# Decoder on one Trainium2 core: row sends spaced out, routing of the last two batches in a stage of its own, x transposed in place, one of five block copies on VectorE

## The chip, the cores and the metric

The kernel runs on one core of one Trainium2 chip. The metric is the device time of one execution, in microseconds (us). The engines are TensorE (PE for matmuls, PEld for weight loads), VectorE (DVE), ScalarE (ACT), GpSimd (POOL) and SyncE (SP, which here only issues DMAs).

## The reference

Two decoder layers with post-layernorm on x of 8 x 512 x 256, float32. The last attention and the mixture of experts, around which the change turns, are:

```python
# layer 0: x = LN(x + attn(x)); x = LN(x + cross(x, ctx)); x = LN(x + butterfly_ffn(x))
# layer 1: x = LN(x + causal_rope_attn(x)); x = LN(x + xattn(x, ctx)); x = LN(x + moe(x))
# xattn: 8 heads of 64; keys and values of x (512) and of ctx (64) joined: 576 keys
sim = jnp.einsum('bihd,bjhd->bhij', q1, k) * scale
attn = jax.nn.softmax(sim, axis=-1)
out = jnp.einsum('bhij,bjhd->bihd', attn, v)
return out.reshape(B, N1, h * d) @ Wo + bo
# moe: 8 experts, the best 2 of each row
xn = (x - mu) * jax.lax.rsqrt(var + EPS) * gamma + beta
logits = jnp.einsum('btd,ed->bte', xn, router_w)
probs = jax.nn.softmax(logits / TEMP, axis=-1)
w, idx = jax.lax.top_k(probs, K)
h = jax.nn.silu(jnp.einsum('btd,edf->betf', xn, W1))
y = jnp.einsum('betf,efd->betd', h, W2)
out = jnp.einsum('bte,betd->btd', wdense, y)      # wdense: softmax weight of the chosen two, else 0
return out + res
```

## The kernel before

x of all eight batches stays in SBUF for the whole kernel (`sh.x_all`, 32 tiles of 128 rows x 256). The stages run one after the other, each a block whose engines all meet at its end: a0 (self attention with decay), x0 (`cross_attention_heads`), f0 (`butterfly_ffn`), a1 (causal attention with rotation), x1 (the last attention), `route`, `experts`, `combine`. a0, a1 and x1 are three kinds of one function, `attention`.

**Steps of x1.** A batch has U = 8 steps: two groups of four heads (G = 2) times four tiles of 128 query rows. Each step handles one tile of one group. TensorE computes its scores (line 878, keys of x, and line 888, keys of ctx); VectorE takes the maximum and moves them to SBUF (lines 1270 and 1279); ScalarE takes the exp, a step later (L1074); TensorE transposes the exps block by block (L901, and L904 for the ctx keys), three steps later (LAG_T); they are copied from PSUM to SBUF, and TensorE multiplies them with the values four steps later (L922, L925) into x_O. In x1 a head has five blocks of transposes per step (T_UNIT = 5: four of 128 keys and one of 64), and ScalarE copies all five (L1065). In a0 and a1 there are four blocks, and VectorE copies one of them (L1254).

**The end of a group.** The reciprocals of the sums are transposed by TensorE (L938), copied to rows by VectorE (L1201), written to DRAM and read back, spread over the partitions, by SP (L697, `x_invrep`). At the group's last step VectorE multiplies x_O with x_invrep (L1261, once per group; the one of group 1 of batch b - 1 falls into batch b's early steps, that of group 0 at step 7). Values of the next group are computed at the same place (L814, L823), copied by ScalarE (L1044). The output product is L837, the layernorm L151. Because of the lags, batch b's last products come in batch b + 1's early steps; after the last batch there is a tail of six steps with nothing of its own.

**x in.** TensorE transposes x (L749 in attention) out of a buffer `xin`, into which SP copies the next batch from `x_all` (512 KB) at step 0 (L703); x0 does the same.

**Routing in x1.** Class `Routing`. Batch b - 2 is routed during batch b (b >= 2): `choose` normalises its rows on VectorE (L298), GpSimd scales them by gamma and beta in place (L372, L375), VectorE takes 32 dot products of a row tile with an expert's router row (L306, four tiles x eight experts), the best two (L314 onwards); `tally` counts them on TensorE; `locate` turns counts into slots (L343 to L356) and releases `placed` (L355). Then `send` issues eight indirect DMAs (L382), each writing 128 rows of `xn` to the slots of `moe_sent`. There is one buffer `xn`, so the next batch's normalising waits until the eight sends have arrived. GpSimd's queue is this loop and nothing else: scale b, send b, scale b + 1, ... for b = 0 to 6. The order on VectorE is that of a generator: `advance(routed[1])` runs one piece of the routing at set places of the steps.

**Tail and route.** Batch 6 is chosen in x1's tail, and located behind it (`advance(ro.locate(...))` at the end of attention). `route` does batch 7: choose (L2029 is its first instruction), tally, locate, send; then it computes each expert's tiles and the slots to gather from, while SP loads the experts' weights (16 transfers of 1 MB, L2007 and L2008). `experts` fetches its first rows at L2136 and multiplies from L2166 on.

## Time and profile before

| | us |
|---|---|
| runs | 4067.27, 4079.03, 4083.48 |
| median | 4079.03 |
| profiled execution | 4074.16, its span 4072.4 |

| stage | from | to | us |
|---|---|---|---|
| a0 | 0 | 835 | 835 |
| x0 | 835 | 1090 | 255 |
| f0 | 1090 | 1336 | 246 |
| a1 | 1336 | 2409 | 1073 |
| x1 | 2409 | 3300 | 891 |
| route | 3300 | 3370 | 70 |
| experts | 3370 | 3953 | 583 |
| combine | 3953 | 4072 | 119 |

Over the span TensorE is busy 3337.6 us (82%), its weight loads 2459.7 (60%), VectorE 2328.9 (57%), ScalarE 1891.7 (46%) and GpSimd 953.4 (23%); the mean granted clock of TensorE is 0.919. The loads of `xin` are 16 transfers of 512 KB in a0 and a1 (4.4 us from issue to landing), and 16 in x0 and x1 (4.2 us).

How to read the views: a row of the timeline has the start (us), the duration (us), engine and line, the operation, output<-inputs, their shapes, the number of instructions in the row, and in brackets the idle time of the engine ahead of it with what ended it: "<-remote" names no instruction, "<-issue" means that the profile shows nothing that was waited for, "<-PEq" TensorE's sequencer. SPq and POOLq are DMA issues. A row of busy time by window has the window, its length, then PE, PEld, DVE, ACT and POOL busy time, each with its count of instructions, the granted TensorE clock (PEclk, as a share of full speed), the mean busy share of the DMA engines, and GB/s. Names begin with the stage (x_ is x0's or x1's, a_ is a0's or a1's, moe_ is the routing's).

### The profile page before, as it was taken

To read this page: it belongs to the slowest core of one execution; us is meant where nothing else is said; L and a number is where in the kernel's file an instruction comes from. 1 tells how busy PE (TensorE), PEld (TensorE's weight loads), DVE (VectorE), ACT (ScalarE), POOL (GpSimd) and SP (SyncE) were. 2 spreads that over 40 slices of the span, in tenths; PEclk is the share of its full clock that TensorE was granted. 3 is DMA by queue.
4 is the path that set the end of the run, shared out by engine and by line. 5 is a ranking of instruction groups with operands and counts; after the bars stand their busy time and mean duration, and the time that the engine had idled before them with its cause. 6 is when DMAs were issued, how large, how long until landed. Compare 5 with 4: busy or idle time off the path is not lost. (4 is left out here: it accounts for less than half of the span.)

```text
span 4072.4 us, 74256 instructions
## 1 busy us (share of the span) xinstructions
PE 3337.6 (82%) x25588; PEld 2459.7 (60%) x25588; DVE 2328.9 (57%) x7554; ACT 1891.7 (46%) x4610; POOL 953.4 (23%) x758
## 2 busy tenths in 40 slices
PE   5888888857699588889889869998888818999970
PEld 3656565647678366666566646776666616776750
DVE  4777777769777356565666634566666652222226
ACT  4777878723332255555555526554555501112110
POOL 0000000034100576676666700011011120000014
PEclk9999999978799799999999979999999969999995
DMA  3111111010200222122221220000000041111113
GB/s 117 53 68 67 67 54 65 7 48 21 97 1 1 82 64 56 48 58 57 58 56 49 55 68 12 18 27 28 28 28 23 22 174 47 33 33 34 34 41 109
DMA packets 115308, 204.35 MB, mean 50 GB/s; under 512 B 23744, under 2 KB 66176, under 8 KB 110080
## 3 DMA queue, kind: packets, MB, share of 16 engines
q1 hardware_dynamic: 104048, 148.21, 12.5%
q0 software_dynamic: 10896, 51.39, 3.4%
q8 instruction: 216, 3.54, 0.4%
q14 instruction: 148, 1.21, 0.1%
HBM read 91.92 MB, written 57.28 MB: 37 GB/s over the span
## 5 line engine op out<-in xcount | busy, mean ns | idle before, releaser
L1074 ACT ACTIVATE a_t<-a_t,a_neg 128x512 f32<-128x512 f32 (+3 forms) x1024 | 642.7, 633 | 9.4 <-DVE a_neg L1284 8.4
L901 PE MATMUL a_T<-ident,a_t 128*128 128x128 f32 x3328 | 512.0, 288 | 126.8 <-ACT a_pT L1065 57.1
L901 PEld LDWEIGHTS a_T<-ident,a_t 128*128 128x128 f32 x3328 | 384.1, 146 | 324.1 <-issue 291.4
L1065 ACT ACTIVATE a_pT<-a_T 128x512 f32<-128x512 f32 (+3 forms) x768 | 370.6, 512 | 273.0 <-PE a_T L901 272.9
L1279 DVE CUSTOM_DVE_ANT_0 a_t<-a_A,a_decay 128x512 f32<-128x512 f32 x512 | 323.0, 687 | 100.6 <-PE a_A L866 100.5
L1279 DVE CUSTOM_DVE_ANT_0 a_t<-a_A,a_table 128x384 f32<-128x384 f32 (+3 forms) x512 | 220.9, 486 | 165.6 <-PE a_A L878 164.3
L1115 POOL TENSOR_TENSOR a_rsin<-a_rawswapped,a_sin 128x512 f32<-128x512 f32 x128 | 168.9, 1319 | 561.0 <-DMA a_rawswapped<-a_raw 547.6
L2236 DVE COPY experts_y<-experts_Y 128x256 f32<-128x256 f32 x72 | 30.5, 424 | 438.2 <-PE experts_Y L2174 438.2
L2186 PE MATMUL experts_H<-ex_w,experts_xgT 128*128 x576 | 261.8, 597 | 0.8 <-ACT experts_xgT L2213 0.6
L2174 PE MATMUL experts_Y<-ex_w,experts_hT 128*128 x1152 | 260.5, 379 | 1.0 <-DVE experts_hT L2245 1.0
L1065 ACT ACTIVATE x_pT<-x_T 128x512 f32<-128x512 f32 (+1 forms) x320 | 178.5, 593 | 169.1 <-PE x_T L901 149.7
L2174 PEld LDWEIGHTS experts_Y<-ex_w,experts_hT 128*128 128x128 f32 x1152 | 218.8, 190 | 61.3 <-issue 35.2
L1279 DVE CUSTOM_DVE_ANT_0 x_t<-x_A,x_table,x_mx 128x512 f32<-128x512 f32 x256 | 177.6, 747 | 133.4 <-PE x_A L878 132.7
L2277 POOL DMA_INDIRECT combine_got<-moe_results,moe_fetch x64 | 62.2, 972 | 628.8 <-PEq L2255 593.0
L1254 DVE COPY a_pT<-a_T 128x512 f32<-128x512 f32 (+3 forms) x256 | 148.2, 579 | 94.3 <-PE a_T L901 92.9
L2219 ACT ACTIVATE experts_h<-experts_H 128x512 f32<-128x512 f32 x144 | 86.0, 597 | 241.1 <-PE experts_H L2186 241.1
L1074 ACT ACTIVATION_READ_ACCUMULATOR a_t<-a_t,a_neg 128x1 f32 x1024 | 196.6, 192 | 0.0
L1074 ACT ACTIVATE x_t<-x_t,x_neg 128x576 f32<-128x576 f32 x256 | 194.7, 765 | 0.0
L837 PE MATMUL a_A<-a_wo,a_oT 128*128 128x256 f32 x640 | 166.4, 413 | 31.7 <-DVE a_mx L1279 22.9
L382 POOL DMA_INDIRECT moe_sent<-moe_xn,moe_place x64 | 62.9, 983 | 495.0 <-issue 424.3
L922 PEld LDWEIGHTS a_O<-a_pT,a_v 128*64 128x64 f32 x2560 | 138.2, 137 | 66.5 <-ACT a_pT L1065 41.3
L878 PE MATMUL a_A<-a_khl,a_qhl 64*128 64x128 f32 (+3 forms) x1536 | 157.3, 336 | 22.2 <-POOL a_khl L1125 19.1
(297 smaller groups left out, 6853.3 us busy)
## 6 DMA issues: line engine op xcount, KB each, us to landing
moe_sent<-a_zeros POOLq DMA_DIRECT2D x33, 1024.0 KB, 8.4
a_rawswapped<-a_raw SPq DMA_DIRECT2D x512, 64.0 KB, 2.0
a_invrep<-a_inv_dram SPq DMA_DIRECT2D x64, 256.0 KB, 4.0
ex_w<-in_f_w_dram SPq DMA_DIRECT2D x16, 1024.0 KB
experts_xg<-moe_sent SPq DMA_DIRECT2D x72, 128.0 KB, 2.0
moe_results<-experts_y SPq DMA_DIRECT2D x72, 128.0 KB, 1.7
a_xin<-x_all SPq DMA_DIRECT2D x16, 512.0 KB, 4.4
x_xin<-x_all SPq DMA_DIRECT2D x16, 512.0 KB, 4.2
```

The lines of the kernel that those rows point to most:

```text
L837: mm = pe.matmul(bank[:, 0:D], oT[:, t, qt * P:(qt + 1) * P], wo[:, t, :], start=(t == 0), stop=(t == n_o - 1))
L878: mm = pe.matmul(A[seg.bank(at)][:, 0:keys(u)], q_hl[r, gp, ql, j // 2, q], k_hl[r, gp, kl_, j // 2, 0:keys(u)], start=(n == 0), stop=(n = ...
L901: mm = pe.transpose(bank[:, kt, :], t_of(u, j, kt * P, (kt + 1) * P), sh.ident[:])
L922: mm = pe.matmul(O[pr][64 * half:64 * half + 64, q], v_sb[:, kt, col], p_tile(u, j, kt), start=(kt == 0), stop=last, skip_group_check=True)
L1065: nc.scalar.activation(to, of, ACT.Copy).then_inc(t_empty, 1)
L1074: nc.scalar.activation(t_of(u_e % U, j, 0, n), t_of(u_e % U, j, 0, n), ACT.Exp, bias=neg[:, slot, j:j + 1], scale=SCALE, accum_out=total[: ...
L1115: nc.gpsimd.tensor_tensor(rsin[:], raw_swapped[:, n % 2, :], sin[:], ALU.mult).then_inc(sin_done, 1)
L1254: nc.vector.tensor_copy(p_tile(u, 3, 0, kts), bank[:, 0:kts, :] if kts > 1 else bank[:, 0, :])\
L1279: nc.vector.tensor_tensor_reduce(t_of(s, j, 0, n), A[seg.bank(name)][:, 0:n], table[:, at:at + n], 1.0, mx1[:, slot, j:j + 1] if x1 else L ...
L2174: mm = pe.matmul(Y[parity][:], hT[:, f, :], w2[:, bass.ds(e, 1), f, :].rearrange("p a d -> p (a d)"), start=(f == 0), stop=(f == FT - 1))
L2186: mm = pe.matmul(H[half][:], xgT[:, dt, :], w1[:, bass.ds(e, 1), dt, half * 512:(half + 1) * 512] .rearrange("p a f -> p (a f)"), start=(d ...
L2219: nc.scalar.activation(h[:, half * 512:(half + 1) * 512], H[half][:], ACT.Silu).then_inc(h_act, 1)
```

## The change

**Sends.** `send` is split into `scale` and a `send` of one group of 128 rows. `xn` has two buffers. GpSimd's loop in x1 is now: scale b, then the eight sends of b - 1, one by one, send g only when the exps have come to a set count (`exped >= ((b + 2) * U + 2) * 4 + 3 * g`, so three heads' exps further for each). Batches 0 to 4 are sent in x1.

**Last two batches.** Batch 6 is no longer routed in x1 (`route = x1 and own and b >= 2`, and no `locate` behind the tail). `route` first sends batch 5's rows, then handles 6 and 7 together: it normalises eight tiles into a buffer `xhat`, GpSimd scales them into `rows` (the memory of the router rows), TensorE transposes `xhat` (32 blocks), ScalarE applies gamma and beta while copying (4 instructions of 512 columns), 16 matmuls with eight columns of output give the logits; the slots come from prefix sums in log rounds; sixteen sends follow. Three small loads (gamma, beta, the transposed router) go ahead of the weight loads.

**x in place.** The buffers `xin`, their loads and the waits for them go in a0, a1, x1 and x0; TensorE transposes straight from `x_all`.

**Copies.** In x1 VectorE copies block 3 of five (512 columns, L1254); ScalarE copies the other four. The condition for a bank to be free counts ScalarE's and VectorE's copies apart.

```diff
-        if b:
-            wait_apart(dve, met, (self.arrived, 16 * self.G * b))
+        xn = self.xn[:, b % 2]
+        if b > 1:
+            wait_apart(dve, met, (self.arrived, 16 * self.G * (b - 1)))
...
-    def send(self, pool, met, b):
-
-        nc, G = self.nc, self.G
-        wide = [P, QT, D]
+    def scale(self, pool, met, b, to, xn):
+
+        nc, wide = self.nc, [P, QT, D]
         wait_apart(pool, met, (self.normal, b + 1))
-        nc.gpsimd.tensor_tensor(self.xn[:], self.xn[:], self.gamma[:].unsqueeze(1).to_broadcast(wide),
-                                ALU.mult).then_inc(self.scaled, 1)
+        nc.gpsimd.tensor_tensor(to, xn, self.gamma[:].unsqueeze(1).to_broadcast(wide), ALU.mult).then_inc(self.scaled, 1)
         wait_apart(pool, met, (self.scaled, b + 1))
-        nc.gpsimd.tensor_tensor(self.xn[:], self.xn[:], self.beta[:].unsqueeze(1).to_broadcast(wide),
-                                ALU.add).then_inc(self.rows, 1)
-        wait_apart(pool, met, (self.placed, b + 1))
-        if b:
-            pool.wait_ge(self.arrived, 16 * G * b)
-        for g in range(G):
-            at = b * G + g
-            pool.indirect_dma_start(self.sent, bass.IndirectOffsetOnAxis(ap=self.place[:, at:at + 1], axis=0),
-                                    self.xn[:, g // TOP, :], None).then_inc(self.arrived, 16)
+        nc.gpsimd.tensor_tensor(to, to, self.beta[:].unsqueeze(1).to_broadcast(wide), ALU.add).then_inc(self.rows, 1)
+
+    def send(self, pool, b, g, row):
+
+        at = b * self.G + g
+        pool.indirect_dma_start(self.sent, bass.IndirectOffsetOnAxis(ap=self.place[:, at:at + 1], axis=0),
+                                row, None).then_inc(self.arrived, 16)
...
-                if s == 0 and nxt:
-                    sp.wait_ge(xt_done, b * DT + DT)
-                    sp.dma_start(xin[:], sh.x_all[:, bass.ds(b * QT + QT, QT), :]).then_inc(xin_in, 16)
...
-                            mm = pe.transpose(bank[:, qt * P:(qt + 1) * P], xin[:, qt, dt * P:(dt + 1) * P],
+                            mm = pe.transpose(bank[:, qt * P:(qt + 1) * P], sh.x_all[:, b * QT + qt, dt * P:(dt + 1) * P],
...
-                if x1 and qt == QT - 1 and b >= 2:
+                if x1 and qt == QT - 1 and 2 <= b < B:
...
-                free = [(t_empty, job + 1)] if x1 else \
-                    [(t_copied, ug + 1)] if j == 1 else [(t_empty, ug * 3 + (2, 0, 3, 4)[j])]
+                if x1:
+                    free = [(t_copied, ug + 1)] if j == 0 else [(t_empty, ug * 4 + (0, 2, 3, 4, 5)[j])]
+                else:
+                    free = [(t_copied, ug + 1)] if j == 1 else [(t_empty, ug * 3 + (2, 0, 3, 4)[j])]
...
-                    if do_t and j < (T_UNIT if x1 else 3):
+                    if do_t and j < T_UNIT and j != 3:
...
-                for b in range(B - 1):
-                    ro.send(pool, (ready, N_READY), b)
+                for b in range(B - 2):
+                    ro.scale(pool, (ready, N_READY), b, ro.xn[:, b % 2], ro.xn[:, b % 2])
+                    for g in range(Routing.G if b else 0):
+
+                        if g == 0:
+                            wait_apart(pool, (ready, N_READY), (ro.placed, b))
+                            if b > 1:
+                                pool.wait_ge(ro.arrived, 16 * Routing.G * (b - 1))
+                        pool.wait_ge(exped, ((b + 2) * U + 2) * 4 + 3 * g)
+                        ro.send(pool, b - 1, g, ro.xn[:, (b - 1) % 2, g // TOP, :])
...
-                route = x1 and b >= 2
+                route = x1 and own and b >= 2
...
-                if not x1 and s < U and (own if u_t >= 0 else prev):
+                if s < U and (own if u_t >= 0 else prev):
                     u = u_t % U
                     wait_apart(dve, (ready, N_READY), (pv, b * U + (u_t + 1)),
                                (t_full, (b * U + u_t) * T_UNIT + (4 + T_CREDIT)))
-                    kts, bank = keys(u) // P, T[(u * T_UNIT + 3) % 2]
+                    kts, bank = S // P if x1 else keys(u) // P, T[(u * T_UNIT + 3) % 2]
...
-                advance(ro.locate(nc.vector, routed[0], B - 2))
...
+        xhat = sb("xhat", [P, LQ, D])
+        rows = ro.router
...
+            pe.wait_ge(loaded, 16 * LOADS)
+            for b in range(LAST):
+                pe.wait_ge(ro.normal, FIRST + b + 1)
+                for dt in range(DT):
+                    for qt in range(QT):
+                        mm = pe.transpose(X[b * DT + dt][:, qt, :], xhat[:, b * QT + qt, dt * P:(dt + 1) * P], sh.ident[:])
+                    mm.then_inc(xt_full, 1)
+            for b in range(LAST):
+                pe.wait_ge(xt_done, (b + 1) * DT)
+                for qt in range(QT):
+                    for dt in range(DT):
+                        mm = pe.matmul(R[:, b * QT + qt, :], xn_T[:, b, dt, qt * P:(qt + 1) * P], router[:, dt, :],
+                                       start=(dt == 0), stop=(dt == DT - 1))
+            mm.then_inc(logits, 1)
+            pe.wait_ge(ro.chose, FIRST + 1)
+            of = chosen[:].rearrange("p g e -> p (g e)")
+            pe.matmul(BEFORE[:].rearrange("p g e -> p (g e)"), ro.tri[:], of, start=True, stop=True)
+            pe.matmul(TOTAL[:].rearrange("p g e -> p (g e)"), ro.ones[:], of, start=True, stop=True).then_inc(counted, 1)
 
         @block.scalar
         def _(act):
+            act.wait_ge(loaded, 16 * LOADS)
+            for b in range(LAST):
+                for dt in range(DT):
+                    act.wait_ge(xt_full, b * DT + dt + 1)
+                    nc.scalar.activation(xn_T[:, b, dt, :], X[b * DT + dt][:].rearrange("p a b -> p (a b)"), ACT.Identity,
+                                         bias=beta[:, dt:dt + 1], scale=gamma[:, dt:dt + 1]).then_inc(xt_done, 1)
             act.wait_ge(shifted, 1)
             nc.scalar.activation(ro.packed[:], ro.packed[:], ACT.Exp).then_inc(exped, 1)
 
         @block.gpsimd
         def _(pool):
             pool.wait_ge(ready, 1)
-            ro.send(pool, (ready, 1), B - 1)
+            wait_apart(pool, (ready, 1), (ro.placed, FIRST))
+            pool.wait_ge(ro.arrived, 16 * G * (FIRST - 1))
+            for g in range(G):
+                ro.send(pool, FIRST - 1, g, ro.xn[:, (FIRST - 1) % 2, g // TOP, :])
+            for b in range(LAST):
+                r = slice(b * QT, (b + 1) * QT)
+                ro.scale(pool, (ready, 1), FIRST + b, rows[:, r, :], xhat[:, r, :])
+            wait_apart(pool, (ready, 1), (ro.rows, B), (ro.placed, FIRST + 1))
+            for b in range(LAST):
+                for g in range(G):
+                    ro.send(pool, FIRST + b, g, rows[:, b * QT + g // TOP, :])
             pool.wait_ge(ro.arrived, 16 * GROUPS)
 
         @block.vector
         def _(dve):
             nv = nc.vector
-            nv.memset(ro.scratch[:], 0.0).then_inc(ready, 1)
+            nv.memset(scratch[:], 0.0).then_inc(ready, 1)
             dve.wait_ge(ready, 1)
             steps = ro.steps(dve, (ready, 1))
-            advance(ro.choose(dve, nv, sh.x_all, steps, (ready, 1), B - 1))
+            for t in range(LQ):
+                ins = nv.bn_stats(stats[:, t, :], sh.x_all[:, FIRST * QT + t, :])
+            steps.link(ins)
+            for t in range(LQ):
+                ins = nv.bn_aggr(mv[:, t, :], stats[:, t, :])
+            steps.mark(ins)
+            advance(rsqrt_columns(nv, steps, mv[:, :, 1], scratch))
+            steps.settle()
+            for b in range(LAST):
+                for qt in range(QT):
+                    t = b * QT + qt
+                    ins = nv.tensor_scalar(xhat[:, t, :], sh.x_all[:, FIRST * QT + t, :], mv[:, t, 0:1],
+                                           scratch[:, 1, t:t + 1], ALU.subtract, ALU.mult)
+                ins.then_inc(ro.normal, 1)
+            dve.wait_ge(logits, 1)
+            steps.link(nv.tensor_scalar(logit[:], R[:], 1.0 / ro.TEMP, None, ALU.mult))
+            for t in range(LQ):
+                ins = nv.max(best[:, t, :], logit[:, t, :])
+            steps.link(ins)
+            for t in range(LQ):
+                ins = nv.max_index(index[:, t, :], best[:, t, :], logit[:, t, :])
+            steps.link(ins)
+            steps.link(nv.tensor_copy(picked[:].rearrange("p (t k) -> p t k", k=TOP), index[:, :, 0:TOP]))
+            by_group = [P, LG, NE]
+            nv.tensor_tensor(chosen[:], picked[:].unsqueeze(2).to_broadcast(by_group),
+                             ro.iota[:, 0:NE].unsqueeze(1).to_broadcast(by_group), ALU.is_equal).then_inc(ro.chose, 1)
+            nv.tensor_copy(ro.packed[:, FIRST * QT:, 0:NE], logit[:])
+            nv.tensor_copy(ro.packed[:, FIRST * QT:, NE:], best[:, :, 0:TOP])
             dve.wait_ge(counted, 1)
-            steps.mark(nv.tensor_copy(ro.count[:].rearrange("p a g e -> p (a g e)"), C[:]))
-            advance(ro.locate(nv, steps, B - 1))
+            nv.tensor_copy(upto[0][:, 0, :], ro.upto[:, 0, :])
+            steps.link(nv.tensor_copy(upto[0][:, 1:, :], TOTAL[:]))
+            at, d = 0, 1
+            while d <= LG:
+                a, c = upto[at], upto[1 - at]
+                nv.tensor_tensor(c[:, d:, :], a[:, d:, :], a[:, :LG + 1 - d, :], ALU.add)
+                steps.link(nv.tensor_copy(c[:, :d, :], a[:, :d, :]))
+                at, d = 1 - at, 2 * d
+            sofar = upto[at]
+            steps.link(nv.tensor_tensor(sums[:], BEFORE[:], sofar[:, 0:LG, :], ALU.add))
+            steps.link(nv.tensor_tensor(sums[:], sums[:], chosen[:], ALU.mult))
+            steps.link(nv.tensor_reduce(picked[:], sums[:], AX_X, ALU.add))
+            nv.tensor_copy(ro.place[:, FIRST * G:], picked[:]).then_inc(ro.placed, 1)
+            steps.link(nv.tensor_copy(small[:, 0, :], sofar[:, LG, :]))
```

## Rows read from the trace of the kernel before

**Rows 1.** Busy time by stage, x1; columns are explained above.
```profile
2409.00:3300.00 891.00, 765.52 (x6112) 585.46 (x6112) 526.86 (x2399) 450.78 (x1024) 80.12 (x62) 0.93 0.10 28
```

**Rows 2.** Timeline of VectorE, line 1261, one product per batch, x1.
```profile
2607.38 1.29 DVE L1261 TENSOR_TENSOR x_oT<-x_O,x_invrep 128x512 f32<-128x512 f32 x2 [2.12 <-PE x_O L925]
2713.93 1.29 DVE L1261 TENSOR_TENSOR x_oT<-x_O,x_invrep 128x512 f32<-128x512 f32 x2 [6.84 <-remote]
...
3143.61 1.29 DVE L1261 TENSOR_TENSOR x_oT<-x_O,x_invrep 128x512 f32<-128x512 f32 x2 [6.92 <-remote]
3241.90 1.29 DVE L1261 TENSOR_TENSOR x_oT<-x_O,x_invrep 128x512 f32<-128x512 f32 x2 [6.33 <-remote]
```

**Rows 3.** Timeline of all engines, 2705 to 2718, around one of these products.
```profile
2705.08 1.07 POOL L382 DMA_INDIRECT moe_sent<-moe_xn,moe_place  x1 [70.68 <-DVE moe_place L355]
...
2707.97 0.65 PE L925 MATMUL x_O<-x_pT,x_v 64*64 64x128 f32 x8
...
2714.13 0.97 POOL L382 DMA_INDIRECT moe_sent<-moe_xn,moe_place  x1 [0.30 <-issue]
...
2716.64 1.34 ACT L1044 ACTIVATE x_v<-x_A 128x512 f32<-128x512 f32 x3 [10.49 <-remote]
```

**Rows 4.** Waits of TensorE in one batch of x1, 2880.3 to 2987.
```profile
PE x_A L878 <- DVE x_mx L1270: 5.2, 1, 5.2
```

**Rows 5.** Timeline: a copy by VectorE in a1; scores in a step of x1.
```profile
1476.09 0.67 DVE L1254 COPY a_pT<-a_T 128x512 f32<-128x512 f32 x1
...
2630.96 0.22 DVE L1270 CUSTOM_DVE_ANT_0 x_t<-x_A,x_table 128x64 f32<-128x64 f32 x1
...
2632.65 1.66 PE L878 MATMUL x_A<-x_khl,x_qhl 64*128 64x512 f32 x12
```

**Rows 6.** Timeline: end of x1, start of route, start of x1.
```profile
3260.77 0.60 PE L938 MATMUL x_A<-ident,x_inv 128*4 128x128 f32 x4
...
3266.24 0.67 DVE L1201 COPY x_invrows<-x_A 4x512 f32<-4x512 f32 x1
...
3268.43 1.23 SPq L697 DMA_DIRECT2D x_invrep<-x_inv_dram  x2
...
3277.75 1.28 DVE L1261 TENSOR_TENSOR x_oT<-x_O,x_invrep 128x512 f32<-128x512 f32 x2
...
3296.45 1.79 DVE L343 TENSOR_TENSOR moe_upto<-moe_upto,moe_count 128x8 f32<-128x8 f32 x7
...
3300.03 0.17 DVE L356 COPY moe_upto<-moe_upto 128x8 f32<-128x8 f32 x1
...
3315.77 0.07 DVE L2029 MEMSET moe_scratch<- 128x12 f32 x1 [15.57 <-PEq L505]
...
2409.18 0.09 DVE L1143 MEMSET x_inv<- 128x32 f32 x1 [0.64 <-PEq L505]
```

**Rows 7.** Timeline of the stage route; last, a window of it.
```profile
3309.84 0.97 POOL L382 DMA_INDIRECT moe_sent<-moe_xn,moe_place  x1 [0.30 <-issue]
...
3322.64 2.33 POOL L372 TENSOR_TENSOR moe_xn<-moe_xn,moe_gamma 128x1024 f32<-128x1024 f32 x1 [11.83 <-DVE moe_xn L298]
...
3342.33 0.18 DVE L314 TENSOR_SCALAR moe_logit<-moe_logit 128x32 f32<-128x32 f32 x1
...
3350.18 1.15 POOL L382 DMA_INDIRECT moe_sent<-moe_xn,moe_place  x1 [22.72 <-issue]
...
3359.57 1.02 POOL L382 DMA_INDIRECT moe_sent<-moe_xn,moe_place  x1 [0.30 <-issue]
...
3367.48 0.39 SPq L2136 DMA_DIRECT2D experts_xg<-moe_sent  x1
...
3340.00:3350.00 10.00, 1.11 (x4) 0.93 (x4) 6.53 (x46) 0.00 (x0) 0.00 (x0) 0.50 1.06 377
```

**Rows 8.** Timeline of VectorE, line 1261, in two batches of a1.
```profile
1992.78 1.29 DVE L1261 TENSOR_TENSOR a_oT<-a_O,a_invrep 128x512 f32<-128x512 f32 x2 [5.64 <-DMA a_invrep<-a_inv_dram]
...
2246.42 1.29 DVE L1261 TENSOR_TENSOR a_oT<-a_O,a_invrep 128x512 f32<-128x512 f32 x2 [6.06 <-DMA a_invrep<-a_inv_dram]
```

More of the change, by code:

```diff
@@ L1154, in _ @@
             dve.sem_inc(o_empty, 2)
-            if not x1:
-                dve.sem_inc(t_copied, 1)
+            dve.sem_inc(t_copied, 1)
             def low_parts(seg, turn, b, g, i):
@@ L1206, in run @@
                     dve.wait_ge(*seg.full(turn, work))
-                    if x1 and work[1] == QT - 1 and b >= 2:
+                    if x1 and work[1] == QT - 1 and 2 <= b < B:
                         routed[0].mark(nc.vector.tensor_copy(
@@ L1427, in _ @@
             sp.dma_start(mask[:], w["mask"].rearrange("b (q p) n -> p (b q) n", p=P)).then_inc(loaded, 16)
-            for b in range(1, B):
-                sp.wait_ge(x_low, b * DT + 2)
-                sp.dma_start(xin[:], sh.x_all[:, bass.ds(b * QT, QT), :]).then_inc(xin_in, 16)
         @block.tensor
@@ L1987, in route @@
         sb, sem = env.sb, env.sem
-        BQ = B * QT
+        BQ, LAST, G = B * QT, 2, ro.G
+        LQ, LG = LAST * QT, LAST * G
+        FIRST = B - LAST
+        gamma = sb("gamma", [P, DT])
+        beta = sb("beta", [P, DT])
+        router = sb("router", [P, DT, NE])
+        xhat = sb("xhat", [P, LQ, D])
+        rows = ro.router
+        xn_T = sb("xnT", [P, LAST, DT, S])
+        stats = sb("stats", [P, LQ, 6])
+        mv = sb("mv", [P, LQ, 2])
+        scratch = sb("scratch", [P, 3, LQ])
+        logit = sb("logit", [P, LQ, NE])
+        best = sb("best", [P, LQ, 8])
+        index = sb("index", [P, LQ, 8], U32)
+        picked = sb("picked", [P, LG])
+        chosen = sb("chosen", [P, LG, NE])
+        upto = [sb(f"upto{i}", [P, LG + 1, NE]) for i in range(2)]
+        sums = sb("sums", [P, LG, NE])
         total = sb("total", [P, BQ, 1])
@@ L1995, in route @@
         where = sb("where", [P, 2, GROUPS])
-        beyond = sb("beyond", [P, GROUPS, NE - 1])
-        C = env.ps("C", [P, 2 * ro.G * NE])
+        beyond = xn_T[:, 1, 0, 0:GROUPS * (NE - 1)].rearrange("p (g e) -> p g e", e=NE - 1)
+        X = [env.ps(f"X{i}", [P, QT, P]) for i in range(LAST * DT)]
+        R = env.ps("R", [P, LQ, NE])
+        BEFORE = env.ps("before", [P, LG, NE])
+        TOTAL = env.ps("all", [P, LG, NE])
+        loaded = sem("loaded")
         ready = sem("ready")
+        xt_full = sem("xt_full")
+        xt_done = sem("xt_done")
+        logits = sem("logits")
         counted = sem("counted")
```

47 lines of the change are left out of this document (19 added, 28 removed).

## The prediction

> **What bounds the kernel now.** I read the busy time by stage first, then the order in time inside the stages that the change touches. The last attention (x1) takes 891 us, TensorE busy 766 of them [rows 1], so in x1 only what makes TensorE wait, or lengthens the way out of the stage, costs time.
>
> The final product of a head group (VectorE, line 1261), once per batch at its step 7, is a good clock. Batch 1, which routes nothing, is followed by a first interval of 106.55 us; the next four average (3143.61 - 2713.93) / 4 = 107.42 us [rows 2]. In each routed batch this product starts after 6.3 to 6.9 us of idleness that ends "remote" [rows 2]. Look inside one [rows 3]: GpSimd begins eight row sends at 2705.08, the last at 2714.13. TensorE ends the x_O matmuls that the product needs at 2708.62 (2707.97 + 0.65), but VectorE starts only at 2713.93 [rows 2], 5.3 us late; ScalarE waits 10.49 us for value matmuls and all three copies then run at once. So **a burst of eight sends holds back what TensorE reports as finished**. Without the hold the first interval would have been 2708.62 - 2607.38 = 101.24 us.
>
> At the end of x1 the reader should see three delays in a row [rows 6]: the reciprocal rows are transposed by 3261.37, but VectorE, busy with routing dot products, copies them at 3266.24 and makes the last product at 3277.75; then it locates batch 6's rows (3296.45 to 3300.20, the end of its last copy); then it idles 15.57 us, because GpSimd still issues sends until 3310.81 [rows 7], and the block ends when all are done. The way into x1 itself cost 0.64 us [rows 6].
>
> **The change, part by part.**
>
> *Sends spaced.* Six bursts (batches 2 to 7) go. One is worth the mean interval less the interval without a hold, 107.42 - 101.24 = 6.2 us at most and 5.3 by the late start alone; the last of them stands in the tail, where I take 4. Sum **-35**, bounds 5 x 5.3 = -26 and 6 x 6.2 = -37. What is late next is the 5.2 us that TensorE waits for VectorE's dot products [rows 4], which stays. Added are 40 sends, each alone behind three exps (some 8 us apart). Each waits in GpSimd's queue ahead of the next batch's scaling, whose input is only ready at step 1 of the next batch, so nobody waits for that. What one send alone does to TensorE's reports is not in the trace; below, nothing; above, 2.5 us, an estimate of how long its data is under way: from the end of the burst's first issue (2705.08 + 1.07 = 2706.15) to the first report that is held (2708.62). A gain is excluded, since a send only adds work. I take 0.05 each, **+2**, nearest to the row of the matmuls at 2707.97, which run with two sends out: the copies that they need had been asked for by TensorE and made [rows 3].
>
> The Trainium skill, DMA: Bandwidth & Descriptors, Queues, rings and completion order, says that each DMA engine takes turns between queues packet by packet, so a burst on GpSimd's queue should cost others only a share of the transfer engines. By that rule spacing would give nothing beyond shorter transfers; the row above disagrees, since what was late was a report of TensorE, not a transfer.
>
> *One of five blocks copied by VectorE.* 8 batches x 8 steps = 64 copies of 512 columns leave ScalarE and come to VectorE at 0.67 us [rows 5]. In an ordinary step VectorE ends its first scores at 2631.18 while TensorE asks at 2632.65, 1.5 us of slack [rows 5], so 0.67 hides. It doesn't where TensorE already waits for VectorE, one step, perhaps two, in each of six routed batches [rows 4]: 6 x 0.67 x 1.5 = **+6**, bounds +2 to +43 (all 64). A gain from the lighter ScalarE I count only in the last steps.
>
> *Last two batches in a stage of their own.* Batch 6 is no longer routed in x1's tail. The rows of reciprocals are copied at 3261.4 instead of 3266.24, the spread is issued 2.2 us later [rows 6] and, as in a1, where the wait for it is 5.64 to 6.06 us [rows 8], lands in some 5, so the last product starts at 3268.6 instead of 3277.75: **-9.1**. Locating goes: 3300.20 - 3296.45 = **-3.8**. The idle time between the stages shrinks from 15.57 to 0.64: **-14.9**, as GpSimd's last send in x1 leaves when the tail starts. TensorE waits less before its last matmuls and ScalarE has a copy less in each tail step: **-1**. Sum **-28.8**, bounds -20 to -33.
>
> Then the route stage itself, counted from its first VectorE instruction, 3315.77. Before: scaling starts at +6.9, logits are ready at +26.6, the sends start at +34.4 and end at +44.8, and the first expert rows are fetched at +51.7 [rows 6, 7]. After: GpSimd first sends batch 5's eight (until +11) and scales two batches (two instructions of 2.33 us each and the step between, 4.9 us, until +21) [rows 7]. VectorE normalises eight tiles instead of four, done at +10 instead of +6.9. Transposes, four ScalarE copies and 16 narrow matmuls replace 32 dot products; no row shows them, between 3 and 12 us (the upper end with TensorE's reports held by the burst beside it), I take 8, nearest to a held report: +18. From logits to places it was 7.9 us [rows 7] for one batch; with twice the tiles but a scan of five rounds 6 to 12, I take 9: +27. Sixteen sends at 9.39 / 7 = 1.34 us [rows 7] end at +48.4, 3.6 later than before: **+3.6**, bounds -3 to +9. A floor stands beside it: 16.8 MB of weights and 3.1 MB of rows at 377 GB/s [rows 7] are 53 us, and +48.4 + 6.9 = 55 lies just above.
>
> *x in place.* 32 transfers of 512 KB go, and TensorE's wait for them. In the batches this gives nothing I can point to: the wait for the spread that the transfer could slow was 5.64 us beside such a transfer and 6.06 us in the batch that has none [rows 8]. At four stage starts 0.5 MB less comes first in the queue, 1.4 us at 377 GB/s where the loads are waited for: 0 to 5.6, I take **-2.5**. The transposes read the same values at the same time as before, so nothing new waits.
>
> **Sum.** -35 + 2 + 6 - 28.8 + 3.6 - 2.5 = -54.7 us. Against the profiled execution (4074.2 us, span 4072.4) this gives 4019.5; the median of the runs shown is 4.9 us above it. I predict 4020.
>
> **The rivals.**
>
> *A send alone holds reports too* (ends slower). If each of the 40 spaced sends stops TensorE's reports for 2.5 us, the cost is 100 instead of 2: 4118. From 1.4 us per send nothing is gained (56.7 / 40), from 1.9 us the kernel is slower by 0.5%. For it: in a burst a report is held 5 us, longer than any one send. Against: the work before 2707.97 passed [rows 3], and TensorE has most often several steps' inputs ready. 5%.
>
> *The burst is not the cause* or the sends bunch up again behind GpSimd's scaling. Then TensorE stalls as before and only the way out of x1 gains: 4020 + 33 = 4053. For it: the hold is seen only together with the value matmuls of step 7, and "remote" names no releaser. Against: batch 7 has no value matmuls and idles 6.33 us as well [rows 2]. 10%. The rule of the Trainium skill's page on DMA (Queues, rings and completion order) that is weighed above points this way too.
>
> *VectorE becomes the bound.* It is busy 527 of 891 us in x1 [rows 1]; with all 64 copies on the path the cost is 43 instead of 6: 4057. Against: the slack of 1.5 us. 8%.
>
> *The new stage is longer than thought*: +9 instead of +3.6 and the tail at its lower bound, 4034; inside the range. 12%.
>
> **How the numbers follow.** Forecast 4020 with 60%; its own bounds give 4000 to 4040. The four rivals have 5, 10, 8 and 12%; 5% is left for a gain beyond the bounds. Half a percent, about what a measurement of this kernel can tell from no change, is 20 us: faster is below 4059. Range 3998 to 4058: it takes in everything but the slower rival, half of what lies beyond, and some spread of the runs. Faster 0.87, same 0.07, slower 0.06.
>
> **What the profile after would show.** Right: the product at step 7 follows its x_O matmuls within 0.2 us and no idle time ends "remote"; intervals of routed batches near 102; indirect sends 6 to 10 us apart; DVE idle below 1.5 us between x1 and route; first expert rows some 55 us after the route stage starts. The step on the copies is wrong if TensorE's wait for x_mx grows beyond 8 us per batch; the step on sends is wrong if ScalarE or VectorE idle 1 to 2 us after single sends. The whole is wrong if TensorE's reports are late somewhere else, or if the fetch of expert rows comes later than 61 us into the stage.

## The result and the profile after

The changed kernel takes 4009.33 us in the median (4005.56 to 4019.47), the kernel before, timed beside it, 4076.57. The ratio is 0.9841 (95% interval 0.982 to 0.9863), 67 us in the medians; the profiled executions differ by 63.7 us (spans 4072.4 and 4008.7). Of all executions in this document one is left out, of the kernel before on the chip of burst3b: 5348.97 us at a granted clock of 0.599.

A stage starts with VectorE's first instruction, the one whose idle time ends with TensorE's sequencer. These starts, in the timeline of the kernel after, are those of x0, a1, x1 and route:

```profile
830.82 1.87 DVE L1537 MEMSET x_v<- 128x2176 f32 x1 [1.10 <-PEq L502]
...
1333.21 0.11 DVE L1138 MEMSET a_inv<- 128x64 f32 x1 [0.65 <-PEq L1798]
...
2399.84 0.09 DVE L1140 MEMSET x_inv<- 128x32 f32 x1 [0.64 <-PEq L502]
...
3249.73 0.08 DVE L2077 MEMSET route_scratch<- 128x24 f32 x1 [0.64 <-PEq L502]
```

and in the kernel before, for x0 and a1 (for x1 and route they stand in [rows 6]):

```profile
836.27 1.87 DVE L1550 MEMSET x_v<- 128x2176 f32 x1 [1.10 <-PEq L505]
...
1336.75 0.11 DVE L1141 MEMSET a_inv<- 128x64 f32 x1 [0.65 <-PEq L1811]
```

| stretch | before | after | difference |
|---|---|---|---|
| a0 | 836.27 | 830.82 | -5.5 |
| x0 and f0 | 500.48 | 502.39 | +1.9 |
| a1 | 1072.43 | 1066.63 | -5.8 |
| x1, up to the product at step 7 of the last batch | 832.72 | 807.08 | -25.6 |
| from there to the first instruction of route | 73.87 | 42.81 | -31.1 |
| route, up to the fetch of the first expert rows | 51.71 | 56.12 | +4.4 |
| the rest | 704.92 | 702.85 | -2.1 |

So 56.7 of 63.7 us come out of x1 and its end, as forecast, and 9.3 out of the stages ahead of it, where 2.5 were forecast. The busy time of x1 (row as in [rows 1]) shows TensorE 10 us less busy than in [rows 1] with nearly the same matmuls (6108 against 6112), at a granted clock of 0.95 instead of 0.93, and VectorE with 17 us more, the copies less batch 6's routing:

```profile
2400.00:3250.00 850.00, 755.55 (x6108) 578.30 (x6108) 544.15 (x2346) 418.27 (x960) 68.89 (x52) 0.95 0.08 24
```

The product at step 7 and the matmuls ahead of it (answers [rows 2] and [rows 3]):

```profile
2598.49 1.29 DVE L1257 TENSOR_TENSOR x_oT<-x_O,x_invrep 128x512 f32<-128x512 f32 x2 [1.25 <-issue]
...
2700.07 0.65 PE L917 MATMUL x_O<-x_pT,x_v 64*64 64x128 f32 x8
...
2700.82 1.29 DVE L1257 TENSOR_TENSOR x_oT<-x_O,x_invrep 128x512 f32<-128x512 f32 x2 [1.17 <-issue]
...
3110.04 1.29 DVE L1257 TENSOR_TENSOR x_oT<-x_O,x_invrep 128x512 f32<-128x512 f32 x2 [1.16 <-issue]
...
3206.92 1.29 DVE L1257 TENSOR_TENSOR x_oT<-x_O,x_invrep 128x512 f32<-128x512 f32 x2 [2.48 <-PE x_O L917]
...
3231.72 1.29 DVE L1257 TENSOR_TENSOR x_oT<-x_O,x_invrep 128x512 f32<-128x512 f32 x2 [5.82 <-DMA x_invrep<-x_inv_dram]
```

TensorE ends x_O at 2700.72 and VectorE multiplies at 2700.82; before, 5.3 us lay between them. The first interval is 102.33 us instead of 106.55, the next four average (3110.04 - 2700.82) / 4 = 102.31 instead of 107.42. In the tail the last product comes 24.80 us after the one at 3206.92, before it was 35.85.

What TensorE waits for in x1, total, times and longest, before:

```profile
PE x_A L878 <- DVE x_mx L1270: 34.9, 12, 5.3
PE x_A L878 <- ACT x_v L1044: 20.9, 5, 4.4
PE x_A L837 <- DVE x_oT L1261: 11.8, 1, 11.8
```

and after:

```profile
PE x_A L868 <- DVE x_mx L1266: 43.2, 16, 5.8
PE x_A L827 <- DVE x_oT L1257: 2.6, 1, 2.6
```

The wait for x_v, which was the echo of the burst, is gone. The wait for x_oT fell by 9.2 us, which is the reciprocal rows no longer queued behind dot products. The wait for x_mx grew by 8.3: VectorE is later with its scores. (The lists are cut to the waits that are discussed.)

Route (answers [rows 7]), counted from 3249.73:

```profile
3257.11 2.84 DVE L2091 TENSOR_SCALAR route_xhat<-x_all,route_mv,route_scratch 128x256 f32<-128x256 f32 x8
...
3266.00 0.23 DVE L2095 TENSOR_SCALAR route_logit<-route_R 128x64 f32<-128x64 f32 x1 [6.05 <-PE route_R L2039]
...
3276.78 1.04 POOL L379 DMA_INDIRECT moe_sent<-moe_router,moe_place  x1 [6.63 <-DVE moe_place L2121]
...
3296.68 0.97 POOL L379 DMA_INDIRECT moe_sent<-moe_router,moe_place  x1 [0.30 <-issue]
...
3305.85 0.37 SPq L2222 DMA_DIRECT2D experts_xg<-moe_sent  x1
```

And four of a batch's eight spaced sends:

```profile
2736.66 1.75 POOL L379 DMA_INDIRECT moe_sent<-moe_xn,moe_place  x1 [8.71 <-ACT x_t L1063]
...
2758.52 0.99 POOL L379 DMA_INDIRECT moe_sent<-moe_xn,moe_place  x1 [20.11 <-ACT x_t L1063]
...
2780.83 0.97 POOL L379 DMA_INDIRECT moe_sent<-moe_xn,moe_place  x1 [12.68 <-ACT x_t L1063]
...
2783.10 0.97 POOL L379 DMA_INDIRECT moe_sent<-moe_xn,moe_place  x1 [1.30 <-ACT x_t L1063]
```

### The profile page after: what moved, and what is told of

It reads as the page before. It is cut to its first block and busy times, and to the rows that moved or that the text cites. A ratio compares the mean times of both kernels' runs of the same rounds, so it can differ in the third digit from the quotient of the medians.

```text
span 4008.7 us, 74188 instructions
## 1 busy us (share of the span) xinstructions
PE 3337.2 (83%) x25632; PEld 2461.8 (61%) x25632; DVE 2339.1 (58%) x7461; ACT 1862.1 (46%) x4550; POOL 953.6 (24%) x758
## 3 DMA queue, kind: packets, MB, share of 16 engines
q1 hardware_dynamic: 100000, 131.44, 11.3%
q0 software_dynamic: 10896, 51.39, 3.4%
## 5 line engine op out<-in xcount | busy, mean ns | idle before, releaser
L1054 ACT ACTIVATE x_pT<-x_T 128x512 f32<-128x512 f32 (+1 forms) x256 | 145.5, 591 | 188.0 <-PE x_T L893 148.7
L1085 POOL DMA_DIRECT2D moe_sent<-a_zeros x33 | 17.6, 541 | 655.1 <-ACT a_xT L1023 655.1
```

The lines of the kernel that those rows point to most:

```text
L1054: nc.scalar.activation(to, of, ACT.Copy).then_inc(t_empty, 1)
```

## The experiments

Each kernel is the changed one or the one before with an edit. The stages ahead of x1 move between executions by more than some of the effects (a0 took 831 to 851 us in the profiles of kernels that are alike there), so x1 and route are read from their own starts. How far x1 itself moves is seen from the changed kernel and the three below whose bursts cost nothing on their chip: 849.9, 849.5, 849.7 and 848.4. Each x1 is that of one profiled execution, so a difference of 1.5 us or less says nothing. The runs fell on more than one chip, which turned out to matter; for each the time of the last stage, combine, is given, which no edit touches.

**ScalarE copies all five blocks.**

```diff
-                    if do_t and j < T_UNIT and j != 3:
+                    if do_t and j < (T_UNIT if x1 else 3):
-                if s < U and (own if u_t >= 0 else prev):
+                if not x1 and s < U and (own if u_t >= 0 else prev):
```

> The kernel after with one part undone: ScalarE copies all five transposed blocks of a head again. By my prediction VectorE's copy costs 6 us, so this should be some 6 us faster than the changed kernel (4003 against 4009 in time, x1 844 us instead of 850), and the wait of TensorE for x_mx in x1 should fall from 43.2 us back to about 35. Rival: the copy on VectorE relieves ScalarE where TensorE waits for x_pT and x_v, and is a gain; then undoing it makes x1 5 to 10 us longer, with more wait for x_pT or x_v.

Measured: x1 843.5 instead of 849.9, so the copy on VectorE costs 6.4 us; forecast were 6. TensorE's wait for x_mx in x1:

```profile
PE x_A L868 <- DVE x_mx L1268: 36.2, 12, 5.3
```

It falls from 43.2 to 36.2 us, and 16 such waits become 12: the copy costs where TensorE waits for VectorE already, and nowhere else. The time is 4010.63 (4002.55 to 4027.13); the spread of the other stages hides 6 us, so the gain is seen in x1 alone. The rival, relief for ScalarE, falls.

**The burst back at step 7.**

```diff
-                        pool.wait_ge(exped, ((b + 2) * U + 2) * 4 + 3 * g)
+                        if g == 0:
+                            pool.wait_ge(exped, ((b + 2) * U + 6) * 4)
```

> The kernel after, but the eight sends of a batch leave in one burst at step 7, where they stood before; two xn buffers, the stage of its own, the copies and x in place stay. If the burst holds TensorE's reports, each of the five bursts costs 5 to 6 us again: x1 is 25 to 31 us longer (875 to 881), the time about 4037, the product at step 7 again waits over 5 us with no releaser named, and TensorE waits some 4 us for x_v after each. Rival (the burst is not the cause, the gain came from the second xn buffer or the copies): x1 stays at 850 and the time at 4009.

Measured: x1 878.1, 28.2 us longer for five bursts, 5.6 each; time 4044.83 (4035.20 to 4061.01); combine 118.0. Everything else of the change was in place, so the spacing alone is worth 28 us on this chip. Which reports are late differs from what was expected, since this burst begins a little earlier in the step:

```profile
2814.98 1.07 POOL L379 DMA_INDIRECT moe_sent<-moe_xn,moe_place  x1 [66.73 <-ACT x_t L1063]
...
2820.72 0.60 ACT L1054 ACTIVATE x_pT<-x_T 128x512 f32<-128x512 f32 x1 [1.96 <-remote]
...
2821.46 1.03 PE L896 MATMUL x_T<-ident,x_t 128*64 128x128 f32 x4 [2.88 <-issue]
...
2825.08 0.59 ACT L1054 ACTIVATE x_pT<-x_T 64x512 f32<-64x512 f32 x1 [3.76 <-issue]
...
2828.48 1.29 DVE L1258 TENSOR_TENSOR x_oT<-x_O,x_invrep 128x512 f32<-128x512 f32 x2 [4.05 <-PE x_O L917]
```

ScalarE's copies wait 1.96 and 3.76 us and no instruction is named as what ended it, TensorE waits 2.88 for nothing that the profile shows, and the product is late by them. There is no long wait for x_v this time. What is late here are TensorE's reports from some 3 us after the first send on.

The lost time is not all waiting. For the same 6108 matmuls TensorE is busy 772.44 us in x1 instead of 755.55, so 16.9 of the 28.2 us are matmuls that take longer and 11.3 are idle time. The rows behind the burst show it:

```profile
2817.00:2822.00 5.00, 2.12 (x18) 1.83 (x18) 3.99 (x19) 2.08 (x7) 3.78 (x5) 0.92 0.30 106
2822.00:2827.00 5.00, 5.00 (x40) 4.83 (x39) 0.69 (x1) 0.59 (x1) 2.39 (x3) 0.50 0.23 84
...
2823.60 3.98 PE L914 MATMUL x_O<-x_pT,x_v 128*64 128x128 f32 x32
```

TensorE is busy 2.12 of the 5 us in which its reports are late, and in the next 5 us its granted clock is 0.50, the lower of its two levels (1.2 instead of 2.4 GHz); the 32 matmuls of x_O take 3.98 us, in the changed kernel 1.97. So the late reports cost twice here: the wait, and slower matmuls after it.

**No sends in x1.** The first five batches' rows are never sent, and the waits for them are left out.

```diff
-                        ro.send(pool, b - 1, g, ro.xn[:, (b - 1) % 2, g // TOP, :])
+                        pass
```

> The kernel after with the 40 spaced sends of x1 left out, so the rows of the first five batches never reach the experts, which then work on zeros in the same number of tiles; and with the waits for these sends left out. By my prediction one send alone costs 0.05 us: x1 is 2 us shorter at most (848). Rival, a single send holds TensorE's reports for up to 2.5 us and the rest was gained elsewhere: x1 20 to 100 us shorter.

Measured: x1 847.8, 2.1 us shorter than with 40 single sends, 0.05 us each. That is little more than x1 moves by itself, so it says that a send alone costs 0.05 us or nothing. The rival that a send alone holds reports falls. (The time, 4020.39, is above the changed kernel's: x1 starts at 2413.75 in this profile instead of 2399.84, in stages without any edit.)

**x in place alone**, put into the kernel before: the loads of xin and the waits for them go, as in the diff above.

> The kernel before with one part of the change alone: TensorE transposes x straight from x_all in all four attention stages, and the loads of xin go. I predicted -2.5 us, from the starts of stages. The traces of before and after show a0 5.5 us and a1 5.8 us shorter, of which 2.0 and about 2 at their starts. If these are all due to x in place, this kernel is 9 to 11 us faster than before (4066); if only the starts are and the rest is the granted clock falling at other places in one execution, 3 to 5 us faster (4073).

Measured: 4064.93 against 4071.15 us, ratio 0.9982 (0.9966 to 0.9997), so 6 us, between 1 and 14. In the profile a1 is 1062.2 us instead of 1072.4, but a0 839.4 instead of 836.3. x1 gains nothing (906.7 against 906.6). In all the profiles with x in place a1 takes 1062 to 1069 us; of the kernel without there is one. And 7.9 of the 10.2 us in a1 are TensorE busy time (900.29 against 908.20 us for the same 6756 matmuls), which is 900 to 913 us in the profiles with x in place, so it moves by itself; TensorE's idle time is 161.9 against 164.2 us. VectorE's wait for the spread reciprocals in a1 (total, times, longest), before:

```profile
DVE a_oT L1261 <- DMA a_invrep<-a_inv_dram: 73.0, 18, 6.1
```

and with x in place:

```profile
DVE a_oT L1254 <- DMA a_invrep<-a_inv_dram: 68.6, 18, 5.6
```

In the changed kernel, nosend and burst7, all with x in place, the same wait is 70.1, 70.1 and 72.5 us, so these 4.4 us are not told from what moves by itself. Where in the stages the 6 us arise stays open.

**Another place, other sizes.** Three kernels, first on one chip (the edits in short form):

```diff
 burst3:  if g == 0:      pool.wait_ge(exped, ((b + 2) * U + 2) * 4)
 fours:   if g % 4 == 0:  pool.wait_ge(exped, ((b + 2) * U + 2) * 4 + 4 * g)
 thin:    burst at step 7; sent = self.sent.rearrange("s (a c) -> (s a) c", c=16); row = row[:, 0:16]
```

> The kernel after, the eight sends of a batch in one burst after step 2, where no values are projected and no head group ends. If a burst holds TensorE's reports wherever it stands, x1 is 20 to 31 us longer than the 850 of the changed kernel, as with the burst at step 7 (878), and waits with no releaser stand some 3 to 11 us behind each first send. Rival: the burst hurts only beside the value projections and the end of a head group at step 7; then x1 is 850 to 855.

> The kernel after, the sends in two bursts of four for each batch. In the kernel before the reports were late from some 3 us after the first issue until all eight were out. If it is the number in flight that counts, a burst of four, 5 us of issues, holds reports for 1 to 2 us: ten bursts, x1 860 to 870. If each send costs the same wherever it stands, 28 / 40 us, it would be 878 as with eight. Rival: a burst has to be longer than four to hold anything: 850.

> The kernel with bursts of eight at step 7 (x1 878.1), each row sent in x1 cut from 1024 bytes to 64, so the experts get only a part of the first five batches' rows, in wrong places. The number of descriptors and GpSimd's work for them are the same. If the bytes written hold TensorE's reports, the hold goes: x1 850 to 855. If the descriptors do, or the work that writes them, it stays: 873 to 881.

Measured: x1 849.5, 849.7 and 848.4 us, all as if there were no burst; times 3994.05, 3997.59 and 3997.02. But the kernel before took 4020.44 there (4009.62 to 4031.41), 51 us less than on the chip of the runs above, and combine took 98.7, 98.7 and 98.6 us in these three instead of 118. So the same three kernels ran once more, and fell on another chip, where the kernel before takes 4062.7 (median of nine, 4056.81 to 4085.2):

> The same kernel as burst3: eight sends in one burst after step 2. On the chip of burst3 the kernel before took 4020 us instead of 4071, the last stage 98.7 us instead of 118, and no report was late. If that is a trait of the chip, then on a chip whose last stage takes 118 us this kernel's x1 is 20 to 31 us longer than 850, with reports late some 3 us behind the first send of each burst; and if this chip's last stage takes 98.6 again, x1 is 849.5 again. Rival: the place of the burst decides, not the chip, and x1 is 850 with a last stage of 118.

> The same kernel as thin: bursts of eight at step 7 with rows of 64 bytes instead of 1024, a part of the first five batches' rows in wrong places. On a chip whose last stage takes 118 us: x1 850 to 855 if the bytes written delay the reports, 873 to 881 if the descriptors and their making do. On a chip whose last stage takes 98.6 us it tells nothing new (848).

> The same kernel as fours: two bursts of four sends for each batch. On a chip whose last stage takes 118 us: x1 860 to 870 if reports are late only while more than two or so sends are out, 878 if every send of a burst costs the same, 850 if four are too few to delay anything.

| kernel | x1 | over 849.9 | over the same kernel on the first chip | combine |
|---|---|---|---|---|
| burst3b: eight after step 2 | 854.1 | +4.2 | +4.6 | 115.9 |
| fours_b: twice four | 863.3 | +13.4 | +13.6 | 113.7 |
| thinb: eight at step 7, 64 bytes a row | 878.3 | +28.4 | +29.9 | 115.6 |
| burst7: eight at step 7, 1024 bytes | 878.1 | +28.2 | not run there | 118.0 |

The first chip is that of burst3, and burst7 ran on a third one. On which chip the changed kernel's 849.9 was taken is not on record. best, below, ran on the chip of burst3b, and its 842.4 with the 6.4 of the copies gives 848.8, so 849.9 fits that chip within about a microsecond.

Three things follow. **The bytes don't matter**: with a sixteenth of them the cost is the same, so it lies with the descriptors or what makes them. (It is not quite the same number of packets: from the totals of GpSimd's DMA queue, 10896 with full rows, 10256 with thin ones and 8976 without the 40 sends, a send has 48 packets with 1024 bytes a row and 32 with 64. GpSimd's time for a send is the same, 0.97 to 1.07 us.) thinb shows the same picture as burst7:

```profile
2796.12 1.07 POOL L382 DMA_INDIRECT moe_sent<-moe_xn,moe_place  x1 [66.67 <-ACT x_t L1066]
...
2802.57 1.03 PE L899 MATMUL x_T<-ident,x_t 128*64 128x128 f32 x4 [2.85 <-issue]
...
2806.12 0.59 ACT L1057 ACTIVATE x_pT<-x_T 64x512 f32<-64x512 f32 x1 [3.69 <-remote]
```

**What a burst costs goes by the place.** In burst3b:

```profile
2944.95 1.01 POOL L379 DMA_INDIRECT moe_sent<-moe_xn,moe_place  x1 [8.61 <-ACT x_t L1063]
...
2950.30 1.65 PE L868 MATMUL x_A<-x_khl,x_qhl 64*128 64x512 f32 x6 [5.82 <-DVE x_mx L1267]
...
2953.09 0.60 ACT L1054 ACTIVATE x_pT<-x_T 128x512 f32<-128x512 f32 x1 [8.94 <-issue]
2955.76 0.60 ACT L1054 ACTIVATE x_pT<-x_T 128x512 f32<-128x512 f32 x1 [2.08 <-PE x_T L893]
```

and burst3, the same kernel on the other chip, at the same place:

```profile
2952.01 0.60 ACT L1054 ACTIVATE x_pT<-x_T 128x512 f32<-128x512 f32 x1 [8.95 <-PE x_T L893]
2952.81 0.60 ACT L1054 ACTIVATE x_pT<-x_T 128x512 f32<-128x512 f32 x1 [0.20 <-PE x_T L893]
```

The burst begins at 2944.95, and until 2950.30 TensorE waits 5.82 us for x_mx, behind VectorE's dot products: for most of the burst it has nothing to report. ScalarE's idle 8.94 us are no sign of a late report, though no releaser is named, since they are 8.95 on the other chip. The first late one is behind the next copy, 2.08 us instead of 0.20, some 10 us after the first send. So reports are late here too, but later and less, and a burst costs 0.8 us instead of 5.6. My expectation of 20 to 31 was wrong, and so was "some 3 us behind the first send"; the rival, that the place decides, is right about the cost. That it is the wait for x_mx which covers the burst is read from these rows, and was not tried by itself.

**Four are enough** to delay a report where work waits for it, as in this second four of a batch:

```profile
2796.50 0.97 POOL L379 DMA_INDIRECT moe_sent<-moe_xn,moe_place  x1 [51.61 <-ACT x_t L1063]
...
2802.40 0.71 ACT L1008 ACTIVATE x_kctx<-x_A 64x64 fp32r<-64x64 f32 x3 [2.66 <-remote]
...
2804.11 1.03 PE L896 MATMUL x_T<-ident,x_t 128*64 128x128 f32 x4 [3.40 <-ACT x_pT L1054]
```

ScalarE waits 2.66 us, TensorE 3.40 for ScalarE. 13.4 us for five batches, 2.7 per batch, about half of what eight cost at step 7. The first four of a batch stand after step 2, where a burst costs little, so it is mostly the second four that are paid for.

**The chip.** The last stage, which issues 64 gathers in one long row, shows the same trait where TensorE does nothing. Between these two rows of the layernorm VectorE's small operations wait for each other's reports only. Changed kernel:

```profile
3921.33 0.25 DVE L145 BATCH_NORM_AGGREGATE combine_mv<-combine_stats 128x2 f32<-128x6 f32 x2 [2.13 <-remote]
...
3936.65 1.38 DVE L151 TENSOR_SCALAR x_all<-x_all,combine_mv,combine_scratch 128x256 f32<-128x256 f32 x4
```

burst3, on the chip where the kernel before takes 4020:

```profile
3920.95 0.25 DVE L145 BATCH_NORM_AGGREGATE combine_mv<-combine_stats 128x2 f32<-128x6 f32 x2
...
3925.03 1.40 DVE L151 TENSOR_SCALAR x_all<-x_all,combine_mv,combine_scratch 128x256 f32<-128x256 f32 x4
```

15.3 us against 4.1. So on the one chip VectorE's own reports are late too while many indirect DMAs are out, and on that of burst3 none is, in either stage. That the chip makes the difference is seen on one chip against the others; what in it differs isn't known.

**Own stage undone.** Batch 6 in x1's tail, batch 7 alone in route, as before; sends spaced.

```diff
-                route = x1 and own and b >= 2
+                route = x1 and b >= 2
+                advance(ro.locate(nc.vector, routed[0], B - 2))
...
```

> The kernel after with the stage of its own undone: batch 6 is routed in x1's tail and located behind it, batch 7 alone in the stage route; sends stay spaced up to batch 4, batch 5's go in a burst as x1's exps end and batch 6's in one behind the tail. I predicted 28.8 us less for x1's end and 3.6 more for the stage: so x1 878 to 883 and route 50 to 52, the time some 25 us longer than the changed kernel's (4034). Rival: with spaced sends the tail is no longer held up and the way out costs only the locating and the last burst: 10 to 15 us longer (4022).

Measured, on the chip without late reports: x1 and what lies behind it 880.0, route 51.4 (to the fetch of the first expert rows), together 931.3. burst3 on the same chip has 849.5 and 56.0, together 905.5: the stage of its own is worth 25.8 us; forecast were 28.8 - 3.6 = 25.2. The idle time ahead of route is 15.55 us again, 0.64 with the stage. The time is 4016.93 (ratio to the kernel before 0.9993, 0.9976 to 1.001): on this chip all the rest of the change comes to nothing measurable.

**A version to beat both**: five copies on ScalarE, and batch 5's sends in x1's tail.

```diff
+                for g in range(Routing.G):
+                    pool.wait_ge(exped, B * U * 4)
+                    pool.wait_ge(ro.arrived, 16 * (Routing.G * (B - 3) + g))
+                    ro.send(pool, B - 3, g, ro.xn[:, (B - 3) % 2, g // TOP, :])
...
```

> The kernel after with two further edits: ScalarE copies all five blocks (x1 6.4 us shorter, as measured), and batch 5's eight sends leave in x1's tail, each once the one before has arrived, instead of at the head of the stage route. x1 843.5, or 2 to 4 us more if these sends delay the tail; route 52 to 54 instead of 56 (the eight sends' 1 MB no longer shares the transfers with the weights), if the places and sixteen sends still set its end. Together 6 to 9 us less than the changed kernel in x1 and route. Rival: the sends in the tail outlast it, and x1 is 3 us or more longer.

Measured: x1 842.4, route 57.0 (changed kernel 56.1, act5 57.2); time 4003.11 (3999.65 to 4018.05), ratio to the kernel before 0.9864 (0.9841 to 0.9887), which doesn't tell it from the changed kernel. x1 got what was expected; route got nothing:

```profile
3212.32 0.97 POOL L379 DMA_INDIRECT moe_sent<-moe_xn,moe_place  x1 [2.22 <-DMA moe_sent<-moe_xn,moe_place]
...
3248.30 6.87 DVE L2095 TENSOR_SCALAR route_xhat<-x_all,route_mv,route_scratch 128x256 f32<-128x256 f32 x8
...
3249.86 2.35 POOL L372 TENSOR_TENSOR moe_router<-route_xhat,moe_gamma 128x1024 f32<-128x1024 f32 x1 [15.61 <-DVE route_xhat L2095]
...
3255.23 1.11 PE L2040 MATMUL route_X<-ident,route_xhat 128*128 128x128 f32 x4 [3.46 <-DVE route_xhat L2095]
...
3273.01 1.04 POOL L379 DMA_INDIRECT moe_sent<-moe_router,moe_place  x1 [12.84 <-DVE moe_place L2125]
```

The sends in the tail leave 3.2 us apart and delay nothing. But GpSimd, now with nothing to send first, starts to scale batch 6's rows at 3249.86, when VectorE is halfway through normalising: its eight instructions take 6.87 us instead of 2.84, and TensorE gets batch 7 only at 3255.23. The first send of the two batches leaves 32.0 us into the stage instead of 27.0 and the last is out at +52.7 instead of +47.9, but the first fetch comes 4.3 us behind it instead of 8.2: the shorter wait behind the sends was used up by their later start. The eight sends at the head of route had kept GpSimd off until VectorE was done. The Trainium skill, SBUF — State Buffer, SBUF: two separate sides, says that VectorE and GpSimd share one pair of ports, and that when VectorE's operation is in a two-port mode or has two inputs in SBUF, whichever of the two starts first locks it for its whole instruction. The trace agrees in the sizes: VectorE's row (3248.30 to 3255.17) covers GpSimd's two instructions (3249.86 to 3254.70, 4.7 us) and is 4.0 us longer than in the changed kernel, and TensorE's second half comes behind them. Whether this VectorE instruction ran in such a mode no run shows, and the order of the two engines was not tried by itself.

## Why the prediction was right, point by point

*A burst of eight holds what TensorE reports.* Right on the chips on which the trace of before was taken and the comparison was made, and shown by undoing it: 5.6 us a burst, inside the bounds of 5.3 and 6.2. Undone was the spacing alone, so the second buffer and the copies are not the cause. But the prediction took the cost for waiting alone; in burst7 16.9 of the 28.2 us are matmuls that take longer, with the clock at its lower level behind a hold, and the price was right because it was read from whole intervals, which hold both. The interval that it took for one without a hold, 101.24, is met without VectorE's copy: (3108.48 - 2705.22) / 4 = 100.8 in act5. Not foreseen: on another chip there is no hold at all, and there only the way out of x1 gains, as the 10% rival had it for another reason.

*One send alone*: +2 forecast, 2.1 measured. The price was a choice near nothing, taken from what passed unhindered ahead of the hold; that it is met to 0.1 us is luck, since x1 moves by 1.5 us between kernels that are alike in cost.

*The sends leave 6 to 10 us apart*: wrong. They are 2.3 to 22 us apart, because exps of one step come together. It cost nothing; two sends 2.3 us apart delay nothing either.

*Copies*: +6 forecast, 6.4 measured, and at the place that was named, where TensorE waits for x_mx already.

*The end of x1*: -28.8, and 4 for the burst in it, against -31.1 measured. The pieces: the last product, -9.1 and the burst's 4 and 1 for the tail's copies, measured -11.1 in all, 3 less; locating, -3.8 forecast, from the product to the stage's end 5.1 less; idle time between the stages, -14.9 forecast and measured.

*Route*: +3.6 forecast, +4.4 measured. Rows normalised at +10 (measured 10.2), logits at +18 (16.3), first send of the two batches at +27 (27.0), last send done at +48.4 (47.9), first fetch 6.9 behind it (8.2). The bound for the transposes with held reports was not needed. (The trace shows 16 transposes of 128x128 in this stage, not the 32 blocks named in the description of the change.)

*x in place*: -2.5 forecast, bounds 0 to -5.6; if a term was mis-sized, it is this one. Alone it gave 6 us (1 to 14), which does not exclude the forecast, and the stages ahead of x1 were 9.3 us shorter in the profile. The step in doubt is "in the batches this gives nothing I can point to", argued from two waits, 5.64 and 6.06 us [rows 8]; over all of a1 the wait for the spread was 73.0 us before and 68.6 to 72.5 with x in place. That the 512 KB transfers slow these spreads is not shown; of the 9.3 us, the 5.5 in a0 are nearly all TensorE busy time (690.79 against 685.94 us for the same 7788 matmuls), which moves between executions.

Sum: x1 up to the product at step 7 of the last batch -25.6 against -23 forecast, the end -31.1 against -32.8, route +4.4 against +3.6, stages ahead -9.3 against -2.5, the rest -2.1 against nothing.

What stays open: what in the chip delays the reports. Neither the bytes nor TensorE are needed for it; indirect DMAs issued back to back and the chip are. Why it begins 3 us behind the first send at step 7 and some 10 behind it after step 2 was not tried either. On the chip without it the changed kernel was not run. From the kernels with bursts that cost nothing there, 3994 to 3998 us in single runs against 4020, its gain is some 25 us there (an estimate), nearly all from the stage of its own (25.8).

## What to carry to other kernels

Idle time that ends with no releaser, with the matmuls waited for long done, is worth a look at what GpSimd issues at that moment; compare with a run where nothing is late before calling it late (8.94 and 8.95 us above); a burst of indirect DMAs can be spread out at 0.05 us each or less, or moved to a place where the engine that would suffer is waiting anyway. An engine kept busy with something harmless can be what protects its neighbour: take it away and look at who starts earlier. A stall of TensorE is paid for twice where its clock falls behind it, so look at the granted clock after a wait too. Read small effects from the stage's own start and end, and look at a stage that no edit touches before comparing runs of two chips.

## What was not expected of the hardware

- Reports of finished work, TensorE's and VectorE's own, come 2 to 5 us late while GpSimd issues four or more indirect DMAs back to back, whether they write 64 or 1024 bytes a row: +28.4 and +28.2 us for five bursts. Of the 28.2, 16.9 are matmuls that take longer; the clock granted in the 5 us behind one hold was 0.50.
- This depends on the chip: x1 with thin bursts of eight at step 7 took 878.3 on one and 848.4 on another, combine 115.6 and 98.6, the kernel before 4062.7 and 4020.4.
- Beside two GpSimd two-operand instructions of together 4.7 us VectorE's normalising gets little done: eight instructions of 256 columns took 6.87 instead of 2.84 us.
